# Attention and routed feed-forward on one core: probabilities turned by VectorE in 32x32 blocks, value product in pieces on 32x64 tiles

## The chip, the core and the metric

The kernel runs on 1 core of one Trainium2 chip. The metric is the time of the whole program on the device in microseconds (us), the median of several runs. In the profile PE is TensorE (products; PEld is its weight loads), DVE is VectorE, ACT is ScalarE, POOL is GpSimd and SP is SyncE, which issues the transfers (DMAs).

## What is computed

The input is x of shape (4, 1024, 256) in float32: four batches of 1024 tokens. One attention layer and one routed feed-forward layer (FFN) are applied, each to the layer-normalized x and added to it. The change concerns the attention:

```
q = x @ Wqa @ Wqb                      # 16 heads of 192 = 128 + 64 (rope)
ckv = x @ Wkva                         # 64 latent + 64 rope columns, shared by the heads
kv = compressed @ Wkvb                 # per head 128 key and 128 value columns
q_pe, k_pe = _rope(q_pe), _rope(k_pe)  # o1 = x1*cos - x2*sin, o2 = x1*sin + x2*cos
scores = qf @ kf^T / sqrt(192), causal
attn = softmax(scores)
out = (attn @ v) @ Wout
```

## The kernel before, in words

**Stages.** `attention_prepare` makes keys, latent values and weights of all batches and stores what doesn't fit (0 to 71 us of the span). `attention` runs from 71 to 1231 us. `ffn` runs from there to the end. The change touches the attention and the hand-over to the FFN.

**Folded weights.** The key and value weights are folded into the queries' and the output weights, so a head's queries are 128 numbers (64 latent, 64 rope), and its values are the 64 latent numbers of a token, the same for all heads. Matrices that need more than one pass of precision are split into a high and a low part: a score product is three products (qh with kTh, qh with kTl, ql with kTh).

**Pairs and bodies.** The work goes by pairs of heads: 8 pairs in each of 4 batches, 32 pairs. `run(r)` on each engine is the body of pair r; bodies go from -1 to 32, the last (LAST = 32) being the tail. A pair's queries are split into two halves c (512 tokens each) and two heads a. Half c=0 sees 4 blocks of 128 keys at most, half c=1 sees 8. In a body every engine does a list of jobs in an order written out by hand (TENSOR, VECTOR, SCALAR, POOL, and FIRST and LAST versions for the first body and the tail). The engines meet by semaphores. `age` tells which pair a job in body r belongs to: queries of half 0 are made for pair r+1; turned probabilities, value product and output of half 1 belong to pair r-1.

**Jobs of a pair**, with the lines of the profile:
- Q (4): queries of a half and head, 2 products of 512 columns (L1202). ROT on DVE: one product with cosT (L1369) and two of 32 partitions each with sinT, which swap the rope halves by reading 32 partitions and writing 32 others (L1371). ADD on POOL sums them (L1454); HIGH on ACT makes qh (L1299), LOW on POOL makes ql (L1461).
- S (16): the scores of a tile of 128 queries against w keys, w = 128, 256, 384, 512 in half 0 and 640, 768, 896, 1024 in half 1, so 2560 and 6656 columns, 9216 in all per pair (L1219). MAX on DVE adds the mask and takes the row minimum of the negated scores (L1357), in place in PSUM. EXP on ACT writes `probs` and the row sums (L1307).
- T: TensorE turns `probs` in 128x128 blocks against the identity, 72 blocks per pair (L1233), into 3 PSUM banks, and OUT copies them to `pT` in SBUF (24 copies per pair, 15 by ACT, L1318, and 9 by DVE, L1382).
- PV: the value product in tiles of 128 rows by 64 columns, the two heads side by side (L1253): 24 products per pair of up to 512 columns, each two records in the profile. Half 1 goes in two parts, half 0 in one.
- INV, spread_inverses and O: DVE inverts the row sums and turns them (L1389, L1392). SP writes them to DRAM in 4 small transfers (L1107) and reads them back spread over partitions in 2 (L1111). DVE multiplies the value product by them (L1400); OHIGH (L1325) and OLOW (L1468) split the result.
- Y (4) and ACC (4): the output product, 6 products of 256 columns each (L1266), added to `acc` by DVE (L1409).

**PSUM.** Scores, queries and output products share banks 0 to 3, turned probabilities banks 4 to 6, the value product bank 7.

**Transfers.** SP also loads weights of the next pair, keys and values of batches 2 and 3, and moves `acc` out and in by halves at a batch's end. Toward the end it loads the first expert weights; POOL splits them into high and low (`split_first_quad`, L633, L635).

## Time and profile before

| | us |
|---|---|
| median of 3 runs (1732.09 to 1732.58) | 1732.47 |
| the profiled execution's own time | 1732.48 |
| its span | 1730.7 |
| PE busy | 1662.5 (96%) |
| DVE busy | 1248.5 (72%) |
| ACT busy | 955.1 (55%) |
| POOL busy | 509.9 (29%) |

The profiled execution ran like the timed ones, and 1.8 us of it lie outside the span. Busy times are unions of an engine's records. A TensorE record holds the time from its start to its last result, so consecutive records overlap, and what a product costs is the distance of two starts. An engine that is not the bottleneck may be idle at no cost. Stretches are given in us from the start of the span.

### The profile page before, as it was taken

The page shows a single profiled execution, that of the slowest core. Times are in us where ns is not written, and L with a number is a line of the kernel's source. Part 1 is how long each engine was busy: PE and PEld are TensorE (multiplying, and loading weights), DVE is VectorE, ACT ScalarE, POOL GpSimd, SP SyncE. Part 2 cuts the span into 40 slices and gives each one's busy share as a digit, 9 for nine tenths or more (in the row PEclk, how much of TensorE's full clock was granted, in tenths as well). Part 3 has the DMA queues.
Part 4 walks back from the last instruction along what each step waited for, and adds up shares of the span by engine and source line. Part 5 has one row for each costly group of instructions (what it writes and reads, how often), then busy time and mean ns, then how long its engine had stood idle before and what let it go on. Part 6 is the DMA issues. An engine that isn't in the chain of part 4 may idle for free.

```text
span 1730.7 us, 31809 instructions
## 1 busy us (share of the span) xinstructions
PE 1662.5 (96%) x11024; PEld 1357.5 (78%) x11024; DVE 1248.5 (72%) x2923; ACT 955.1 (55%) x2255; POOL 509.9 (29%) x433
## 2 busy tenths in 40 slices
PE   5799999999999999999999999999999999999998
PEld 4667777777777777777777777777699999999998
DVE  6888888888888788888888888888654554555543
ACT  6566666666666666666666666666433333433332
POOL 4543334323333333423343333335310110110100
PEclk9899999999999999999999999999999999999999
DMA  8300010012000003000002210001300000000000
GB/s 287 117 26 20 20 32 25 20 47 96 20 25 20 20 32 111 26 20 26 25 26 65 65 32 24 22 19 38 110 1 25 26 1 25 26 14 12 13 13 13
DMA packets 50204, 68.49 MB, mean 40 GB/s; under 512 B 8512, under 2 KB 33088, under 8 KB 50048
## 3 DMA queue, kind: packets, MB, share of 16 engines
q1 hardware_dynamic: 50048, 66.45, 11.6%
q8 instruction: 93, 1.52, 0.4%
q14 instruction: 63, 0.52, 0.1%
HBM read 52.00 MB, written 14.42 MB: 38 GB/s over the span
## 4 chain that ended last, share of the span: by engine, by line
PE 81%; issue 8%; DVE 4%; ACT 2%; DMA 1%; POOL 1%; ACTq 0%; DVEq 0%
PE aps L43 46%; PE fps L43 23%; PE aps L1233 9%; PE fps L1618 2%; ACT probs L1307 1%; DVE f_stats L739 1%; DMA raw_down<-in_down 1%; DVE nmax L1357 0%; POOL rot L1454 0%; PE fps L700 0%; PE fps L668 0%; DVE aTl L1759 0%; DVE rot L1371 0%; DVE aps L1357 0%; DVE rot L792 0%
## 5 line engine op out<-in xcount | busy, mean ns | idle before, releaser
L1307 ACT ACTIVATE probs<-aps,nmax 128x384 f32<-128x384 f32 (+7 forms) x512 | 378.6, 743 | 229.7 <-DVE nmax L1357 224.0
L1357 DVE CUSTOM_DVE_ANT_0 aps<-aps,mask_row 128x384 f32<-128x384 f32 (+7 forms) x512 | 387.2, 772 | 105.9 <-PE aps L43 100.3
L1233 PE MATMUL aps<-ident,probs 128*128 128x128 f32 x2304 | 324.0, 272 | 0.9 <-ACT probs L1307 0.6
L43 PE MATMUL aps<-kTh,qh 128*128 128x512 f32 (+3 forms) x768 | 293.3, 382 | 23.3 <-ACT probs L1307 18.4
L1233 PEld LDWEIGHTS aps<-ident,probs 128*128 128x128 f32 x2304 | 271.7, 140 | 27.2 <-issue 1.5
L1318 ACT COPY pT<-aps 128x512 f32<-128x512 f32 (+3 forms) x485 | 229.5, 504 | 92.1 <-PE aps L1233 89.5
L43 PE MATMUL aps<-pT,v 128*64 128x512 f32 (+3 forms) x1536 | 268.9, 492 | 0.6 <-ACT pT L1318 0.6
L43 PE MATMUL aps<-kTl,qh 128*128 128x512 f32 (+3 forms) x768 | 257.9, 343 | 0.0
L1454 POOL TENSOR_TENSOR rot<-rot 64x512 f32<-64x512 f32 x128 | 163.9, 1280 | 211.8 <-DVE rot L1371 211.8
L43 PE MATMUL aps<-kTh,ql 128*128 128x512 f32 (+3 forms) x768 | 221.8, 343 | 0.0
L43 PEld LDWEIGHTS aps<-pT,v 128*64 128x64 f32 x1536 | 101.7, 136 | 152.1 <-issue 142.1
L1461 POOL TENSOR_TENSOR ql<-rot,qh 128x512 fp32r<-128x512 f32 x128 | 164.9, 1288 | 158.5 <-ACT qh L1299 158.5
L43 PEld LDWEIGHTS aps<-kTh,qh 128*128 128x128 f32 x768 | 145.7, 190 | 74.4 <-issue 57.9
L1468 POOL TENSOR_TENSOR ol<-o,oh 128x512 fp32r<-128x512 f32 x64 | 82.3, 1286 | 352.8 <-ACT oh L1325 352.8
L1702 ACT CAST aTh<-fps 128x512 fp32r<-128x512 f32 (+1 forms) x96 | 52.9, 552 | 236.1 <-PE fps L1618 236.0
L1759 DVE TENSOR_TENSOR aTl<-fps,aTh 128x512 fp32r<-128x512 f32 (+1 forms) x96 | 62.0, 647 | 167.3 <-ACT aTh L1702 167.3
L43 PE MATMUL fps<-wth,qh 128*128 128x352 f32 x512 | 176.1, 344 | 2.0 <-PEq L833 2.0
L1371 DVE TENSOR_TENSOR rot<-aps,sinT 32x512 f32<-32x512 f32 x256 | 174.2, 680 | 3.5
L43 PE MATMUL fps<-wtl,qh 128*128 128x352 f32 x512 | 166.3, 325 | 0.0
L43 PE MATMUL fps<-wth,ql 128*128 128x352 f32 x512 | 166.2, 325 | 0.0
L43 PEld LDWEIGHTS aps<-kTl,qh 128*128 128x128 f32 x768 | 146.7, 191 | 9.5
L43 PEld LDWEIGHTS aps<-kTh,ql 128*128 128x128 f32 x768 | 136.7, 190 | 8.2
(190 smaller groups left out, 2878.1 us busy)
## 6 DMA issues: line engine op xcount, KB each, us to landing
linv_b<-inverses_scratch SPq DMA_DIRECT2D x128, 128.0 KB, 2.8
wqs<-wq_scratch SPq DMA_DIRECT2D x30, 256.0 KB, 3.1
raw_numbers<-in_x SPq DMA_DIRECT2D x8, 512.0 KB, 6.2
acc<-in_x SPq DMA_DIRECT2D x8, 512.0 KB, 4.0
inverses_scratch<-linv_t SPq DMA_DIRECT2D x256, 1.0 KB
x_scratch<-acc SPq DMA_DIRECT2D x8, 512.0 KB, 2.9
x<-x_scratch SPq DMA_DIRECT2D x8, 512.0 KB, 3.9
out<-x SPq DMA_DIRECT2D x7, 512.0 KB, 2.9
```

Source lines behind the costliest of these rows:

```text
L43: return nc.tensor.matmul(out, lhsT, rhs, start=start, stop=stop, skip_group_check=True)
L1233: last = nc.tensor.transpose(tps[:, TS.index(x) % 3, j * P:(j + 1) * P], probs[c][:, c * (pair % 2), a, off:off + P], t.ident[:])
L1307: nc.scalar.activation(probs[c][:, c * (r % 2), a, off:off + w], sps[:, at:at + w], ACT.Exp, bias=nmax[:, c, a, j:j + 1], scale=-1.0, accu ...
L1318: nc.scalar.copy(pT[:, k % PT_BUFS, s:QC], tps[:, k % 3, s:QC]).then_inc(t_sb["scalar"], 1)
L1357: nc.vector.tensor_tensor_reduce(out=s, in0=s, in1=mask[:, N - PW[c][j]:N], scale=-1.0, scalar=3.0e38, op0=ALU.add, op1=ALU.min, accum_out ...
L1371: last = nc.vector.tensor_tensor(rot2[to:to + 32, k, :], sps[source:source + 32, at:at + QC], t.sinT[to:to + 32, cols], ALU.mult)
L1454: nc.gpsimd.tensor_tensor(rot1[0:64, k, :], rot1[0:64, k, :], rot2[:, k, :], ALU.add).then_inc(q_add, 1)
L1461: nc.gpsimd.tensor_tensor(ql[:, a, cols], rot1[:, k, :], qh[:, a, cols].bitcast(F32), ALU.subtract).then_inc(q_split, 1)
L1468: nc.gpsimd.tensor_tensor(ol[:, cols], o32[:, c, :], oh[:, cols].bitcast(F32), ALU.subtract).then_inc(o_low, 1)
L1618: last = nc.tensor.transpose(turned_in(i, q)[:, (m - 4 * q) * P:(m - 4 * q + 1) * P], act_sb[:, i % 2, m * P:(m + 1) * P], t.ident[:])
L1702: nc.scalar.copy(aTh[:, i % 2, m.start:m.stop, :].rearrange("p m n -> p (m n)"), turned_in(i, q)[:, 0:len(m) * P]).then_inc(aT_h, 1)
L1759: nc.vector.tensor_tensor(aTl[:, i % 2, m.start:m.stop, :].rearrange("p m n -> p (m n)"), turned_in(i, q)[:, 0:len(m) * P], aTh[:, i % 2, ...
```

## The change

All of `attention` is written anew around these parts; its core is in the diff below.
- **Turning.** T and OUT are gone. After EXP, DVE turns the tile of probabilities in 32x32 blocks (TURN, one instruction per score tile, 16 per pair, 9216 columns). Block b of 32 keys lands in `pT[c][:, a, b, :]` with key k of the block on partition 32g+k, where g tells which 32 of a tile's 128 queries the block holds. `probs` is a ring of 5 tiles, `pT` has one buffer per half for both heads.
- **Value product.** PV runs over blocks of 32 keys. Each block is 8 products: 4 row groups g by 2 heads, with 32 rows, 64 columns of weights and up to 128 columns of moving data. 16 blocks in half 0 and 32 in half 1 give 384 products per pair in place of 24. The result takes 4 banks (4 to 7), one per row group. The values lie four times in SBUF (`vrep`), loaded from DRAM by 4 transfers per batch in runs of 256 bytes. PV(1) is now one stretch, in 4 jobs, and PV(0) in 2.
- **Rope.** ACT copies the queries from PSUM (RAW), SP swaps the two halves of 32 partitions by two transfers (SWAP), and POOL does both multiplications and the sum (ROT). DVE has no part in it.
- **Order.** New lists for all engines, one list for the first body too, SP's jobs in a list of their own (SYNC), and all 8 banks shared by scores, queries and outputs.
- **acc** has two buffers, a whole batch each; it is stored and loaded whole.
- **First expert weights** are split by ACT (high) and DVE (low) in the tail, not by POOL.

```
-KB = [4, 8]
-PT_BUFS = 12
+S32 = 32
+BLOCKS = [16, 32]
+PARTS = [2, 4]
+RING = 5
+OB = 4
...
-                sp.dma_start(t.v_dram[b - 2], t.v32[:, b % 2]).then_inc(kq_stored[b % 2], 16)
+                sp.dma_start(t.v_dram[b].rearrange("(t p) d -> p t d", p=P), t.v32[:, b % 2]).then_inc(kq_stored[b % 2], 16)
...
+        TENSOR = [Q(1, 0), S(0, 1, 0), S(0, 0, 1), Q(1, 1), S(0, 0, 0), S(0, 1, 1), S(0, 1, 2), Q(0, 1), S(0, 1, 3),
+                  Y(0, 1), S(0, 0, 3), S(0, 0, 2), PV(1, 0), PV(1, 1), PV(1, 2), PV(1, 3), S(1, 0, 3), S(1, 0, 1),
+                  S(1, 1, 0), Q(0, 0), Y(0, 0), S(1, 0, 0), S(1, 1, 3), PV(0, 0), PV(0, 1), S(1, 1, 2), S(1, 0, 2),
+                  S(1, 1, 1), Y(1, 0), Y(1, 1)]
+        VECTOR = [MAX(0, 1, 1), MAX(0, 1, 0), MAX(0, 1, 2), MAX(0, 0, 0), MAX(0, 1, 3), ACC(0, 1), INV(1),
+                  TURN(0, 1, 1), TURN(0, 1, 0), MAX(0, 0, 3), MAX(0, 0, 1), TURN(0, 1, 2), MAX(0, 0, 2), INV(0),
+                  TURN(0, 0, 0), TURN(0, 0, 3), TURN(0, 0, 1), O(1), TURN(0, 1, 3), TURN(0, 0, 2), MAX(1, 0, 3),
+                  MAX(1, 0, 1), MAX(1, 1, 0), TURN(1, 0, 3), ACC(0, 0), MAX(1, 0, 0), TURN(1, 1, 0), MAX(1, 1, 3),
+                  TURN(1, 0, 1), TURN(1, 0, 0), TURN(1, 1, 3), O(0), MAX(1, 1, 2), MAX(1, 0, 2), MAX(1, 1, 1),
+                  ACC(1, 0), TURN(1, 0, 2), ACC(1, 1), TURN(1, 1, 2), TURN(1, 1, 1)]
+        POOL = [ROT(1, 0), LOW(1, 0), ROT(1, 1), LOW(1, 1), ROT(0, 1), ROT(0, 0), OLOW(1), LOW(0, 1), LOW(0, 0),
+                OLOW(0)]
+        SYNC = [SWAP(1, 0), SWAP(1, 1), KEEP(1), SPREAD(1), KEEP(0), SPREAD(0), SWAP(0, 1), SWAP(0, 0)]
...
+        TENSOR_FIRST = TENSOR
...
+            def swap(x, r):
+                k = rot_slot(x, r)
+                sp.wait_ge(q_raw, count(of("raw", x), r))
+                sp.dma_start(rot2[0:32, k, :], rot1[32:64, k, :]).then_inc(q_swapped[k], 16)
+                sp.dma_start(rot2[32:64, k, :], rot1[0:32, k, :]).then_inc(q_swapped[k], 16)
...
+            def load_values(b):
+                for a in range(4):
+                    sp.dma_start(vrep[32 * a:32 * a + 32, b % 2], t.v_dram[b].rearrange("(n k) d -> k n d", k=S32))\
+                        .then_inc(values_loaded[b % 2], 16)
...
+                if r == 0:
+                    sp.wait_ge(t.values_stored, 32)
+                    for b in (0, 1):
+                        load_values(b)
+                        load_acc(b)
...
+                if r % PAIRS == 0 and r > 0:
+                    b = r // PAIRS - 1
+                    sp.wait_ge(y_added, last_of("acc", 1, r - 1))
+                    sp.wait_ge(y_added, last_of("acc", 0, r - 1))
+                    sp.dma_start(x2_v[b], acc[:, 1 - b % 2]).then_inc(x2_stored, 16)
+                    if b + 2 < B:
+                        sp.wait_ge(x2_stored, 16 * (b + 1))
+                        load_acc(b + 2)
...
+                def pv_job(x):
+                    _, c, part = x
                     pair = r + age(x)
...
+                        pe.wait_ge(p_turned, last_of("tr", c, pair))
+                        banks_free(x)
+                    n = BLOCKS[c] // PARTS[c]
+                    for b in range(part * n, (part + 1) * n):
+                        s = max(0, b // 4 - 4 * c) * S32
+                        for a in range(4):
+                            for h in range(2):
+                                last = mm(nc, banks[64 * h:64 * h + 64, OB + a, s:4 * S32],
+                                          vrep[32 * a:32 * a + 32, pair // PAIRS % 2, b, :],
+                                          pT[c][32 * a:32 * a + 32, h, b, s:], b == 0, b == BLOCKS[c] - 1)
...
+                def raw_job(x):
+                    _, c, a = x
+                    act.wait_ge(q_ps, count(Q(c, a), r))
...
+                    nc.scalar.copy(rot1[:, rot_slot(x, r), :], banks[:, bank_of(Q(c, a), r), :]).then_inc(q_raw, 1)
...
+                def turn_job(x):
+                    _, c, a, j = x
+                    w = PW[c][j]
+                    dve.wait_ge(e_done, count(EXP(c, a, j), r))
+                    if r > 0:
+                        dve.wait_ge(pv_done, last_of("p", c, r - 1))
+                    nc.vector.transpose(pT[c][:, a, 0:w // S32, j * S32:(j + 1) * S32],
+                                        probs[:, SLOT[EXP(c, a, j), r], 0:w].rearrange("p (b k) -> p b k", k=S32))\
+                        .then_inc(p_turned, 1)
...
-                def add_job(x):
+                def rot_job(x):
                     _, c, a = x
...
+                    pool.wait_ge(q_swapped[k], 32 * ((count(of("raw", x), r) + 1) // 2))
+                    nc.gpsimd.tensor_tensor(rot2[:, k, :], rot2[:, k, :], t.sinT[:, cols], ALU.mult).then_inc(q_turned, 1)
+                    nc.gpsimd.tensor_tensor(rot1[0:64, k, :], rot1[0:64, k, :], t.cosT[0:64, cols], ALU.mult)\
+                        .then_inc(q_turned, 1)
+                    pool.wait_ge(q_turned, 2 * n)
                     nc.gpsimd.tensor_tensor(rot1[0:64, k, :], rot1[0:64, k, :], rot2[:, k, :], ALU.add).then_inc(q_add, 1)
```

## Rows read from the trace of the kernel before

**Rows 1.** The page: busy time of the engines; chain that ended last, by line.

```profile
PE 1662.5 (96%) x11024; PEld 1357.5 (78%) x11024; DVE 1248.5 (72%) x2923; ACT 955.1 (55%) x2255; POOL 509.9 (29%) x433
PE aps L43 46%; PE fps L43 23%; PE aps L1233 9%; PE fps L1618 2%; ACT probs L1307 1%; DVE f_stats L739 1%; DMA raw_down<-in_down 1%; DVE nmax L1357 0%; POOL rot L1454 0%; PE fps L700 0%; PE fps L668 0%; DVE aTl L1759 0%; DVE rot L1371 0%; DVE aps L1357 0%; DVE rot L792 0%
```

**Rows 2.** Stretches: length, busy us (records) of PE, PEld, DVE, ACT, POOL; granted clock, DMA.

```profile
390.85:532.98 142.13, 139.07 (x897) 106.56 (x897) 116.59 (x252) 90.53 (x213) 50.95 (x41) 1.00 0.13 42
...
71.30:106.90 35.60, 27.31 (x136) 20.48 (x137) 28.62 (x65) 18.25 (x45) 16.53 (x15) 0.86 0.18 54
```

**Rows 3.** TensorE in order of time in one period: start us, length us, records.

```profile
501.07 0.60 PE L1233 MATMUL aps<-ident,probs 128*128 128x128 f32 x4
...
506.20 3.65 PE L43 MATMUL aps<-pT,v 128*64 128x512 f32 x16
...
516.59 2.38 PE L43 MATMUL aps<-pT,v 128*64 128x512 f32 x16
...
528.50 2.37 PE L43 MATMUL aps<-pT,v 128*64 128x512 f32 x16
```

**Rows 4.** Groups of DVE, 390.85 to 532.98 us: count, busy us, mean ns, idle before.

```profile
L1357 DVE CUSTOM_DVE_ANT_0 aps<-aps,mask_row 128x896 f32<-128x896 f32 (+6 forms) x64 | 48.4, 772 | 13.3 <-PE aps L43 12.7
L1371 DVE TENSOR_TENSOR rot<-aps,sinT 32x512 f32<-32x512 f32 x32 | 21.8, 680 | 0.4
L1382 DVE COPY pT<-aps 128x384 f32<-128x384 f32 (+3 forms) x36 | 17.6, 507 | 0.1
L1409 DVE TENSOR_TENSOR acc<-aps,acc 128x512 f32<-128x512 f32 x16 | 11.1, 692 | 1.9 <-PE aps L43 1.6
L1369 DVE TENSOR_TENSOR rot<-aps,cosT 128x512 f32<-128x512 f32 x16 | 10.9, 679 | 1.0 <-PE aps L43 1.0
...
L1400 DVE TENSOR_TENSOR o<-aps,linv_b 128x512 f32<-128x512 f32 x8 | 5.5, 692 | 8.3 <-PE aps L43 8.3
L1392 DVE STREAM_TRANSPOSE linv_t<-linv 128x32 f32<-128x32 f32 x8 | 1.7, 212 | 0.3
L1389 DVE RECIPROCAL linv<-lsum 128x8 f32<-128x8 f32 x8 | 1.6, 198 | 0.1
```

**Rows 5.** Groups of DVE by form, whole span: one-source copies and casts.

```profile
L1382 DVE COPY pT<-aps 128x512 f32<-128x512 f32 x64 | 43.7, 683 | 0.0
L1382 DVE COPY pT<-aps 128x128 f32<-128x128 f32 x31 | 8.7, 280 | 0.0
L787 DVE CAST soft_h<-mask_row 128x256 fp32r<-128x256 f32 x8 | 2.4, 294 | 0.3
```

**Rows 6.** Group of PE by form, whole span: products on four row groups (FFN).

```profile
L43 PE MATMUL fps<-mw,xq 32*128 32x352 f32 x256 | 27.7, 423 | 0.0
```

**Rows 7.** TensorE in order of time: products on four column groups, in the tail.

```profile
1225.32 0.80 PE L43 MATMUL aps<-wth,mu 128*32 128x352 f32 x8
```

**Rows 8.** Groups of ACT, 390.85 to 532.98 us.

```profile
L1307 ACT ACTIVATE probs<-aps,nmax 128x896 f32<-128x896 f32 (+6 forms) x64 | 47.3, 743 | 28.9 <-DVE nmax L1357 28.1
L1318 ACT COPY pT<-aps 128x512 f32<-128x512 f32 (+3 forms) x61 | 29.1, 506 | 11.3 <-PE aps L1233 10.9
```

**Rows 9.** Groups of POOL, 390.85 to 532.98 us.

```profile
L1461 POOL TENSOR_TENSOR ql<-rot,qh 128x512 fp32r<-128x512 f32 x16 | 20.6, 1289 | 20.4 <-ACT qh L1299 20.4
L1454 POOL TENSOR_TENSOR rot<-rot 64x512 f32<-64x512 f32 x16 | 20.5, 1280 | 26.3 <-DVE rot L1371 26.3
L1468 POOL TENSOR_TENSOR ol<-o,oh 128x512 fp32r<-128x512 f32 x9 | 11.6, 1287 | 55.0 <-ACT oh L1325 55.0
```

**Rows 10.** SP's transfers of the inverses, 400 to 536 us: issue in ns, landing.

```profile
L1107 SPq DMA_DIRECT2D inverses_scratch<-linv_t x32: 263/295/689, 403.8 to 534.1; - x32
L1111 SPq DMA_DIRECT2D linv_b<-inverses_scratch x18: 450/520/603, 402.6 to 535.8; - x18
...
DMA to landing us min/median/max: 2.7/2.8/3.4
```

**Rows 11.** TensorE in order of time: the first score product of the attention.

```profile
77.55 0.69 PE L43 MATMUL aps<-kTh,qh 128*128 128x384 f32 x1 [4.22 <-POOL ql L1461]
```

More of the change, by code:

```diff
@@ L885, in S, with PV @@
             return ("s", c, a, j)
[L887 to L894 removed]
+        def PV(c, part):
+            return ("p", c, part)
         def Y(c, i):
@@ L903, in EXP, with TURN, RAW, SWAP @@
             return ("exp", c, a, j)
-        def OUT(c, kb, a):
-            return ("out", c, kb, a)
+        def TURN(c, a, j):
+            return ("tr", c, a, j)
+        def RAW(c, a):
+            return ("raw", c, a)
+        def SWAP(c, a):
+            return ("sw", c, a)
         def ROT(c, a):
             return ("rot", c, a)
-        def ADD(c, a):
-            return ("add", c, a)
         def HIGH(c, a):
@@ L921, in INV, with KEEP, SPREAD @@
             return ("inv", c)
+        def KEEP(c):
+            return ("spw", c)
+        def SPREAD(c):
+            return ("spr", c)
         def O(c):
@@ L985, in R @@
+        TENSOR_FIRST = TENSOR
+        VECTOR_FIRST = VECTOR
+        SCALAR_FIRST = SCALAR
+        POOL_FIRST = POOL
+        SYNC_FIRST = SYNC
+        BANK_FIRST = BANK
+        AFTER_EXPERTS = [x for x in VECTOR if x[0] == "max" and x[1] == 1][2]
         def R(part):
@@ L1014, in exists, with body @@
             return 0 <= r + age(x) < B * PAIRS
-        BODIES = range(-1, B * PAIRS + 1)
-        def body(order, first, r):
+        BODIES = range(-1, LAST + 1)
+        def body(order, first, last, r):
+            if r == LAST:
+                return last
             return [x for x in (first if r == 0 else order) if exists(x, r)]
         def tensor_body(r):
-            return body(TENSOR, TENSOR_FIRST, r)
-        TS = [x for x in TENSOR if x[0] == "t"]
-        PVS = [x for x in TENSOR if x[0] == "p"]
@@ new lines, in attention, with of @@
+        SS = [x for x in TENSOR if x[0] == "s"]
+        COUNT, KINDS = {}, {}
+        for bodies in (tensor_body, vector_body, scalar_body, pool_body, sync_body):
+            for r in BODIES:
+                for x in bodies(r):
+                    if x[0] not in ("router", "mask", "stats", "quad"):
+                        KINDS[x[0]] = KINDS.get(x[0], 0) + 1
+                        COUNT[x, r] = KINDS[x[0]]
+        def count(x, r):
+            return COUNT[x, r]
+        def of(kind, x):
+            return (kind,) + x[1:]
@@ new lines, in at_pair, with last_of, slot_before @@
+        def at_pair(x, pair):
+            return count(x, pair - age(x))
+        def last_of(kind, c, pair):
+            return max(at_pair(x, pair) for x in TENSOR + VECTOR + SCALAR if x[0] == kind and x[1] == c)
+        RING_USERS = [(x, r) for r in BODIES for x in scalar_body(r) if x[0] == "exp"]
+        SLOT = {y: n % RING for n, y in enumerate(RING_USERS)}
+        def slot_before(x, r):
+            n = RING_USERS.index((x, r))
+            return RING_USERS[n - RING] if n >= RING else None
@@ L1069, in bank_users, with takes_banks @@
+        def takes_banks(x):
+            return x[0] in ("s", "q", "y", "router", "mask") or x[0] == "p" and x[2] == 0
+        USERS = {bank: [(x, r) for r in BODIES for x in tensor_body(r) if takes_banks(x) and bank in banks_of(x, r)]
+                 for bank in range(8)}
         def bank_users(x, r):
@@ L1295, in high_job @@
                     pair = r + age(x)
-                    act.wait_ge(q_add, count(Q(c, a), r))
+                    act.wait_ge(q_add, count(ROT(c, a), r))
                     if pair > 0:
-                        act.wait_ge(s_ready, count([y for y in SS if y[1:3] == (c, a)][-1], pair - 1))
-                    nc.scalar.copy(qh[:, a, c * QC:(c + 1) * QC], rot1[:, QS.index(Q(c, a)) % 2, :]).then_inc(q_high, 1)
+                        act.wait_ge(s_ready, max(at_pair(y, pair - 1) for y in SS if y[1:3] == (c, a)))
@@ L1350, in max_job @@
                     _, c, a, j = x
-                    at = slot(S(c, a, j), r) + place(c, j)
-                    if r == 0 and x == next(y for y in VECTOR_FIRST if y[0] == "max"):
+                    at = at_of(S(c, a, j), r)
+                    if r == 0 and x == next(y for y in vector_body(0) if y[0] == "max"):
                         dve.wait_ge(mask_loaded, 16)
@@ L1440, in run @@
                         router_vector(nc, t, 0, 0, None)
-                    if r == LAST - 1 and x == MAX(1, 1, 2):
+                    if r == LAST - 1 and x == AFTER_EXPERTS:
                         router_experts(nc, t)
@@ L1477, in run @@
                         router_norm(nc, t, 1, i)
-                for x in body(POOL, POOL_FIRST, r):
+                job = {"rot": rot_job, "low": low_job, "olow": olow_job, "stats": stats_job}
+                for x in pool_body(r):
                     job[x[0]](x)
-                    if r == LAST - 1 and x == LOW(1, 0):
-                        pool.wait_ge(q_ps, max(count(Q(1, a), LAST - PAIRS - 1) for a in range(2)))
+                    if r == LAST - 1 and x == [y for y in pool_body(r) if y[0:2] == ("low", 1)][-1]:
+                        pool.wait_ge(q_ps, max(at_pair(Q(1, a), LAST - PAIRS - 1) for a in range(2)))
                         router_root(nc, t, 0)
```

493 lines of the change are left out of this document (196 added, 297 removed).

## The prediction

> **What bounds the kernel now.** I read the page first: TensorE is busy for 96% of the span, DVE for 72%, and the chain that ended last lies on TensorE's attention products and its turning line L1233 [rows 1]. That points at TensorE, but it is an average over three stages, so I then took a stretch of whole pairs. Four periods lie between 390.85 and 532.98 us, 35.53 us each. In them TensorE is busy 139.07 of 142.13 us, DVE 116.59, ACT 90.53, POOL 50.95, at full granted clock [rows 2]. Per pair that is 34.8 us of TensorE, 29.1 of DVE, 22.6 of ACT, 12.7 of POOL. TensorE idles 0.77 us a pair: it is the bound, and what leaves it shows in the time until the next engine is full. DVE is next, only 6.4 us below the period. About 31 periods repeat this way; the first body and the tail differ.
>
> **TensorE, removed: the turning.** Four blocks span 0.60 us where one lasts 272 ns [rows 3], so a block costs (0.60 - 0.27) / 3 = 0.109 us; 72 a pair are 7.9 us.
>
> **TensorE, changed: the value product.** Its three stretches span 3.65, 2.38 and 2.37 us [rows 3]; less the overlap of each with its successor (about 0.1), 8.2 us. The columns are 9216, two products at a time, so 4608 steps of 1.78 ns. The rest of TensorE's pair is 34.8 - 7.9 - 8.2 = 18.7 us (scores, queries, output) and stays. New, the 384 products have 8 x 1280 + 8 x 3328 = 36864 columns; eight at a time that is again 4608 steps, so 8.2 us. This is the lower end. No row shows eight tiles at once, but four row groups do run together: 256 products in groups of four are busy 27.7 us, 0.433 us a group, where one lasts 0.423 [rows 6]; so the four start within about 10 ns. Four column groups too: 8 records of 352 columns in 0.80 us [rows 7], where eight in a row at 0.8 ns a column would need 2.3. The upper end is that each of the 768 records costs the 0.109 us of a whole turning block: 84 us. I stay near the lower end, since rows 6 and 7 are the nearest, and add 1.3 us for the narrow pieces: the last 16 blocks of each half have 128, 96, 64 and 32 columns, and a 32-column piece (27 ns of streaming a record) can't hide eight starts and weight loads. PV is then 9.5 us, TensorE 28.2 us.
>
> **DVE.** Removed: rope (21.8 + 10.9) and copies 17.6, together 50.3 us in four periods [rows 4], 12.6 a pair. 16.6 us stay, MAX (48.4 / 4 = 12.1) above all. Added: 16 turns of 9216 columns. The trace has this operation only for 32 columns, 212 ns [rows 4]. A one-source copy goes from 280 ns at 128 columns to 683 at 512 [rows 5], 1.05 ns a column. A turn of w columns is so 212 + 1.05 (w - 32): 16 x 178 ns + 9216 x 1.05 ns = 2.8 + 9.7 = 12.5 us. Lower end: SBUF to SBUF at the rate of the cast, 294 ns for 256 columns [rows 5], which leaves about 0.5 ns a column, 7.5 us. Upper end: each 32x32 block costs the full 212 ns, 61 us. I take 12.5, since the copy is the same kind of stream, and no row shows the cast's rate for a turn. DVE is then 29.1 us a pair, as busy as now, but the fullest engine. (The Trainium skill's page "VectorE: DVE Perf Modes", section on the three transpose paths, gives 311 ns for a 128x128 bf16 turn; as an estimate from it and the 212 ns, 1.03 ns a column and 12.4 us. No row here shows a turn of that width.)
>
> **ACT, POOL, SP.** ACT loses 29.1 / 4 = 7.3 us of copies [rows 8] and gains 4 RAW of about 0.6: 17.8 us. POOL gains two multiplications for each ADD, 8 x 1.28 = 10.2 us [rows 9]: 23.0 us. SP issues 8 more transfers a pair at some 0.3 us, landing 2.8 us later [rows 10]; they stand behind the waits of KEEP and SPREAD. All three fit under 31 us, so I cost them nothing in steady state. Their cover is DVE's fullness.
>
> **Period.** DVE needs 29.1 us and TensorE 28.2. TensorE now reaches 98% because the others have slack; two engines this close, in fixed orders, with probabilities in a ring of 5, wait for one another. I take 94% for DVE: 31.0 us. Gain 4.53 x 31 = 140 us.
>
> **Once only.** *Start:* a first score now waits for rope on DVE and one POOL sum, and comes at 77.55 after 4.22 us of TensorE idle [rows 11]. It will wait for RAW 0.6, two issues and landing 3.4, two ROT of 3.84 on POOL (the second queued ahead of LOW) and LOW 1.3, some 7 us more. The granted clock over this body is 0.86 [rows 2], so part of it ran at 1.2 GHz, after TensorE had waited; more waiting keeps it there longer. The first value product also waits for 1024 runs of 256 bytes in each of four transfers, which SP issues only after its jobs of the body. I take +11 us in all (between +3 and +25). *Batch ends:* in bodies 8 and 16 SP waits for the last ACC, stores, waits for the landing (2.8) and loads, and the next SWAP is queued behind; +5 for both (0 to 12). *Tail:* 52 blocks are not turned, -5.6 us; the expert split moves from POOL to ACT and DVE and lies beside the value product, nothing (up to +4). The FFN is unchanged.
>
> **Sum**, against the profiled execution's 1732.48 us (span 1730.7 and 1.8 outside; the median of the runs is the same within 0.01): 1732.5 - 140.4 + 11 + 5 - 5.6 = **1602.5 us**, 7.5% less.
>
> **Rivals.**
> 1. *The query chain holds the body.* Queries of half 1 are made in the body that uses them: Q, RAW, SWAP, three POOL operations, HIGH, LOW come to 0.6 + 3.4 + 3.8 + 0.6 + 1.3 = 9.7 us for the first head, and 5.2 us more on POOL for the second. TensorE's work ahead of S(1,1,0) is about 14 us. There is hardly slack, and SP may be in SPREAD when the swap is due. For it: POOL goes from 36% to 74% of a period. Against: with DVE as bound TensorE is late anyway. Price 2.5 us a pair, 33.5 us: 1732.5 - 63 + 10.4 = 1680.
> 2. *Only four products in flight*, as rows 6 and 7 show and no row exceeds. PV takes 9216 x 1.78 = 16.4 us, TensorE 35.1, the period about 35.9: 1732.5 + 11 + 10.4 = 1754, slower. It decides from PV = 15.7 us on (35.53 - 0.77 - 18.7, less 0.3 for the start).
> 3. *A start costs more than the streaming.* If a record of 32 rows costs a quarter of the 0.109 us of a whole block, 27 ns, PV is 768 x 0.027 = 21 us, the period about 40.5: 1732.5 + 154 + 10 = 1897. The 10 ns for four starts [rows 6] speak against it, but these are bursts of four, not 512 in a row. The turning point is 20 ns a record. Here belongs the rule of the Trainium skill's page "TensorEngine Tiling (Array Packing)", section Performance Considerations, that each matmul has some 60 cycles of overhead: as an estimate 25 ns a record, 19.2 us, and 1842 us in all. By that rule the change loses; rows 6 shows four starts in less than one such overhead.
> 4. *Turning is slower than a copy.* At 2 ns a column TURN is 21 us, DVE 38, the period about 39: 1732.5 + 107 + 10 = 1850. It decides from 18.6 us on, 1.7 ns a column.
> 5. *No net gain*: several delays together use up the 140 us.
>
> **How the numbers follow.** A measurement of this kernel can tell about 0.2% from no change. Forecast 0.60, rival 1 0.22, rival 2 0.05, rival 3 0.05, rival 4 0.04, rival 5 0.04. Faster 0.60 + 0.22 = 0.82, same 0.04, slower 0.14. The forecast's own range is 1565 to 1640. The low end of the whole range is a period of 29.4 us, DVE without a gap: 1732.5 - 190 + 10 = 1552. The high end reaches past rival 1, a period of 34.3: 1732.5 - 38 + 10 = 1705. Rivals 2 to 4 stay outside, 0.14.
>
> **What would show it.** Right: a period near 31 us; DVE over 90% busy in it with 16 turns of 9216 columns in 12 to 13 us; TensorE 75 to 92%; the value product of half 1 spanning 6 to 7.5 us and of half 0 under 3.5. Wrong: a value product over 12 us, with starts of records at an even distance whatever their columns (rival 3) or at twice the streaming time (rival 2); turns of 1024 columns far from 1.25 us (rival 4, or below it a gain); TensorE idle behind POOL's ql (rival 1); granted clock under 1 in the middle of the attention.

## The result and the profile after

The changed kernel takes **1989.04 us** (median of 4 runs, 1983.5 to 1995.41) beside 1732.4 us for the kernel before on the same chip: a ratio of 1.148 (95% interval 1.145 to 1.152). The forecast was 1602.5 us and 7.5% less; it is 14.8% more, above the whole range (1552 to 1705). The profiled execution took 1987.38 us, its span is 1985.6.

From the page of the kernel after (parts 1, 2, 3 and 5, beside [rows 1]); in part 5 the columns are busy us and mean ns, then idle time just before and what ended it:

```profile
span 1985.6 us, 72308 instructions
PE 1614.7 (81%) x31760; PEld 1434.3 (72%) x31760; DVE 1176.2 (59%) x2772; ACT 803.5 (40%) x1902; POOL 812.4 (41%) x681
...
PEclk9889889887998988898889889888889999999999
q8 instruction: 252, 4.13, 0.9%
...
L46 PE MATMUL aps<-pT_second,vrep 32*64 32x128 f32 (+1 forms) x16384 | 255.1, 265 | 182.9 <-issue 174.0
L46 PE MATMUL aps<-pT_first,vrep 32*64 32x128 f32 (+3 forms) x8192 | 120.9, 255 | 87.0 <-issue 78.0
```

No engine is full: TensorE 81%, VectorE 59%. What is new is in the last two rows. In front of the value product TensorE idles 182.9 + 87.0 us, and "issue" ended nearly all of it: neither data nor a semaphore was waited for. The kernel has 72308 instructions (31809 before), and the queue that brings instructions moves 252 packets and 4.13 MB (93 and 1.52 before).

Four periods of the body, against [rows 2]:

```profile
606.30:770.65 164.35, 132.27 (x3489) 115.58 (x3488) 107.44 (x233) 71.45 (x168) 90.21 (x72) 0.91 0.13 35
```

A period is 41.1 us (before 35.5, forecast 31.0). VectorE's 26.9 us, ScalarE's 17.9 and POOL's 22.6 a period are what the change promised, so the parts moved off TensorE arrived where they should. TensorE is the one that is late, and its granted clock is 0.91 where it was 1.00.

TensorE's timeline shows why. One whole value product of half 1 and what follows it (start, length, shape of the first record, count of records; in brackets the idle time before):

```profile
735.13 3.08 PE L46 MATMUL aps<-pT_second,vrep 32*64 32x128 f32 x198 [0.22 <-ACT probs L1331]
739.27 2.06 PE L46 MATMUL aps<-pT_second,vrep 32*64 32x128 f32 x128 [1.06 <-issue]
742.74 1.72 PE L46 MATMUL aps<-pT_second,vrep 32*64 32x96 f32 x128 [1.41 <-issue]
746.21 1.13 PE L46 MATMUL aps<-pT_second,vrep 32*64 32x32 f32 x58 [1.75 <-issue]
747.27 0.80 PE L46 MATMUL aps<-kTh,qh 128*128 128x512 f32 x1
747.86 0.63 PE L46 MATMUL aps<-kTl,qh 128*128 128x512 f32 x1
748.29 0.63 PE L46 MATMUL aps<-kTh,qh 128*128 128x512 f32 x1
```

After the first 198 records the product runs in bursts of exactly 128, and they start 3.47 us apart (739.27, 742.74, 746.21), although the records of the first of them have 128 columns and those of the second 96 and 64. A burst is 128 products and 128 weight loads: 256 instructions. A packet of the instruction queue is 16384 bytes, and 159 more packets for 40499 more instructions are 255 instructions each. In the trace three packets of this queue start at 736.93, 740.39 and 743.81 us, as far apart as the bursts, and each takes about 1 us. The gaps keep their place in the code and not in the work: in five bodies in a row the first one of half 1 stands behind 168, 178, 188, 198 and 208 records. So a burst is a packet, and TensorE eats one in about 2 us and waits for the next. 3.47 us is the shortest of 76 such distances in the run, the median is 4.0. The value product shown takes 12.1 us in half 1 (735.13 to 747.27) and 5.3 in the half 0 before it (716.17 to 721.50); over the four periods it is 18.5 us a pair, of which 7.1 are gaps, where I had put 9.5. (The Trainium skill's page "Vector Engine (DVE) Microarchitecture Reference", section on instruction fetch and dispatch, says that an instruction has 64 bytes; 2.61 MB more for 40499 more instructions are 64.4 bytes, which agrees.)

The last two rows show the second loss. Scores of 512 columns start 0.43 us apart (747.86, 748.29), where they are 0.23 apart after a stretch without gaps (below): 1.2 GHz instead of 2.4, for 3 to 10 us at a time behind or in a value product, in every body. Of the 41.1 us, 18.5 are value product, 18.7 the rest at full clock (the term of the prediction), 0.7 other idle time (32.1 - 29.2 us of issue, over four); so the lower clock takes some 3 us a pair outside the value product. The clock is at 1.2 GHz for 7.7 us a pair in these periods, which can't cost more than 3.8.

```profile
731.41 0.40 PE L46 MATMUL aps<-kTh,qh 128*128 128x512 f32 x1
731.64 0.40 PE L46 MATMUL aps<-kTl,qh 128*128 128x512 f32 x1
```

Over the run: the first maximum comes 8.6 us later than before (the first score product 6.2), the 31 distances from one body's first maximum to the next sum to 1330.2 us (before 1093.1), and what follows is 9.3 us longer; 8.6 + 237.1 + 9.3 = 255.0, the difference of the spans within 0.1. In what follows "the period" is the median of these 31 distances: 41.7 us after, 35.5 before.

VectorE's turns came as worked out:

```profile
L1389 DVE STREAM_TRANSPOSE pT_second<-probs 128x1024 f32<-128x1024 f32 x8 | 9.8, 1222 | 0.0
L1389 DVE STREAM_TRANSPOSE pT_first<-probs 128x128 f32<-128x128 f32 x8 | 2.2, 269 | 0.0
```

### The profile page after: what moved, and what is told of

It reads as the page before. It is cut to its first block, busy times and chain, and to the rows that moved or that the text cites. A ratio compares the mean times of both kernels' runs of the same rounds, so it can differ in the third digit from the quotient of the medians.

```text
span 1985.6 us, 72308 instructions
## 1 busy us (share of the span) xinstructions
PE 1614.7 (81%) x31760; PEld 1434.3 (72%) x31760; DVE 1176.2 (59%) x2772; ACT 803.5 (40%) x1902; POOL 812.4 (41%) x681
## 3 DMA queue, kind: packets, MB, share of 16 engines
q8 instruction: 252, 4.13, 0.9%
## 4 chain that ended last, share of the span: by engine, by line
PE 64%; issue 16%; DVE 11%; DMA 3%; ACT 2%; POOL 1%; SPq 0%; ACTq 0%; DVEq 0%
PE aps L46 41%; PE fps L46 20%; DVE aps L1379 4%; DVE pT_second L1389 3%; PE fps L1632 2%; DVE acc L1423 2%; ACT probs L1331 1%; DMA wqs<-wq_scratch 1%; DMA x_scratch<-acc 1%; DVE nmax L1379 0%; DMA vrep<-values_scratch 0%; DVE f_stats L754 0%; DMA raw_down<-in_down 0%; PE fps L715 0%; PE fps L683 0%
## 5 line engine op out<-in xcount | busy, mean ns | idle before, releaser
L1331 ACT ACTIVATE probs<-aps,nmax 128x256 f32<-128x256 f32 (+7 forms) x512 | 375.0, 740 | 499.3 <-DVE nmax L1379 497.9
L1379 DVE CUSTOM_DVE_ANT_0 aps<-aps,mask_row 128x256 f32<-128x256 f32 (+7 forms) x512 | 376.2, 768 | 157.4 <-PE aps L46 156.4
L46 PE MATMUL aps<-pT_second,vrep 32*64 32x128 f32 (+1 forms) x16384 | 255.1, 265 | 182.9 <-issue 174.0
L1471 POOL TENSOR_TENSOR rot<-rot,sinT 64x512 f32<-64x512 f32 x128 | 162.5, 1270 | 550.5 <-DMA rot<-rot 550.5
L46 PEld LDWEIGHTS aps<-pT_second,vrep 32*64 32x64 f32 x16384 | 232.6, 135 | 211.5 <-issue 208.4
L1389 DVE STREAM_TRANSPOSE pT_second<-probs 128x768 f32<-128x768 f32 (+3 forms) x256 | 254.5, 1023 | 0.3 <-ACT probs L1331 0.3
L1411 DVE TENSOR_TENSOR o<-aps,linv_b 128x512 f32<-128x512 f32 x64 | 44.2, 691 | 319.8 <-PE aps L46 319.8
L46 PE MATMUL aps<-pT_first,vrep 32*64 32x128 f32 (+3 forms) x8192 | 120.9, 255 | 87.0 <-issue 78.0
L46 PEld LDWEIGHTS aps<-pT_first,vrep 32*64 32x64 f32 x8192 | 111.0, 137 | 104.7 <-issue 95.4
L1472 POOL TENSOR_TENSOR rot<-rot,cosT 64x512 f32<-64x512 f32 x128 | 162.8, 1272 | 0.0
```

The costliest lines, as they stand in the source:

```text
L46: return nc.tensor.matmul(out, lhsT, rhs, start=start, stop=stop, skip_group_check=True)
L1331: nc.scalar.activation(probs[:, SLOT[x, r], 0:w], sps[:, at:at + w], ACT.Exp, bias=nmax[:, c, a, j:j + 1], scale=-1.0, accum_out=lsum[:, c ...
L1379: nc.vector.tensor_tensor_reduce(out=s, in0=s, in1=mask[:, N - PW[c][j]:N], scale=-1.0, scalar=3.0e38, op0=ALU.add, op1=ALU.min, accum_out ...
L1389: nc.vector.transpose(pT[c][:, a, 0:w // S32, j * S32:(j + 1) * S32], probs[:, SLOT[EXP(c, a, j), r], 0:w].rearrange("p (b k) -> p b k", k ...
L1411: nc.vector.tensor_tensor(by_token(o32[:, c, :]), banks[:, OB:OB + 4, 0:4 * S32].rearrange("p a (j i) -> p a j i", j=4), by_token(linv_b[: ...
L1471: nc.gpsimd.tensor_tensor(rot2[:, k, :], rot2[:, k, :], t.sinT[:, cols], ALU.mult).then_inc(q_turned, 1)
```

## Experiments

The theories. **A**: TensorE gets its code at 256 instructions per 3.47 us; the value product's 1536 instructions a pair outrun that. **B**: the 27 ns a record are what a record costs to start, wherever it stands (rival 3 of the prediction). **C**: too few products run at once, so streaming bounds (rival 2). **D**: the orders of the other engines set 41 us. Further experiments take up the rope, the ends of the batches, and a version that keeps the gain. A single run of the changed kernel can lie 6 us from its median, so differences under that are not read.

**e_few: 8 of 48 blocks.**

```
 for b in range(part * n, (part + 1) * n):
+    if b > 0 and b % n < n - 1:
+        continue
```

> The value product keeps 8 of its 48 blocks a pair (the first of each half and the last of each part); the other 40 are left out, so it has 256 TensorE instructions instead of 1536. Theory A (code fetch: TensorE gets 256 instructions per 3.47 us in the value product): PV falls from 17.4 to about 3.5 us a pair, the granted clock stays at 1.0, VectorE becomes the bound at 94% and the period is 30 to 32 us, the time 1600 to 1660 us. Rival D (the written order of VectorE, POOL and the transfers sets 41 us, not PV): the period stays 39 to 41 us, the time above 1900 us.

Measured: 1628.31 us, the period 30.3 us. Windows of four periods, and the page's instruction queue (packets, MB, share):

```profile
442.70:564.50 121.80, 95.14 (x930) 77.74 (x929) 106.49 (x235) 71.13 (x168) 90.46 (x72) 0.90 0.16 45
```

```profile
q8 instruction: 92, 1.51, 0.4%
```

D falls: with the value product short, the same orders run at 30 us, within 0.7 us of the forecast of 31.0 for the period. Two expectations were wrong. The clock is 0.90 here too; no loss by it shows, and TensorE is busy only 78%. And VectorE isn't the bound: it is busy 87%, not 94%, and the chain that ended last in these four periods lies mostly on the rope, that is on the swap (14%) and the three operations of ROT on POOL (31%):

```profile
by line: DMA rot<-rot 14.3%; POOL rot L1477 10.5%; POOL rot L1473 10.4%; POOL rot L1474 10.3%; ACT probs L1333 9.7%; issue 9.3%; PE aps L46 7.0%; DVE aps L1381 5.7%; DMA inverses_scratch<-linv_t 3.6%; POOL ql L1483 3.1%; SPq L1129 3.1%; ACT
```

**e_half: 24 of 48 blocks.** The edit skips blocks with `b % 4 in (1, 2)`.

> The value product keeps 24 of its 48 blocks a pair (two of every four are left out), 768 instructions instead of 1536. Theory A (code fetch, 13.6 ns an instruction): PV takes 768 x 13.6 = 10.4 us less what is fetched ahead, TensorE 27 to 29 us, the period 32 to 35 us, the time 1680 to 1790 us. Rival C (only four products in flight, PV bound by streaming 9216 columns at 1.78 ns): PV 8.2 us and 33 to 34 us: not told apart here but by e_narrow. Rival D (orders of the other engines): above 1900 us.

Measured: 1655.8 us, better than the range given; the period is 31.6 us, 156 instruction packets. From 256 to 768 instructions a pair the kernel grows by 27 us, from 768 to 1536 by 333: up to some point the code is there ahead of time or the rope chain covers the wait, from there each instruction is paid for.

**e_narrow: every product, 32 columns each.**

```
+                        e = 4 * S32 if b == 0 else s + S32
...
-                                last = mm(nc, banks[64 * h:64 * h + 64, OB + a, s:4 * S32],
+                                last = mm(nc, banks[64 * h:64 * h + 64, OB + a, s:e],
...
-                                          pT[c][32 * a:32 * a + 32, h, b, s:], b == 0, b == BLOCKS[c] - 1)
+                                          pT[c][32 * a:32 * a + 32, h, b, s:e], b == 0, b == BLOCKS[c] - 1)
```

> All 384 products of a pair stay, but each has 32 columns (the first block of each half keeps 128); the other columns are left out, so streaming falls to 27% of 36864 columns with the same 1536 instructions. Theory A (code fetch): the value product of half 1 still spans 11 to 12.5 us, of half 0 4.5 to 5.5 us, in bursts of 128 records 3.4 to 3.5 us apart, each burst shorter (about 1 us) and the gap longer; the time within 3% of after, 1930 to 2010 us, if anything the clock is lower. Rival C (streaming, four in flight or fewer): PV falls to about a third, the period to 31 us, the time to about 1620 us. Rival B (each record costs 27 ns to start): PV as in A but with starts at an even distance inside a burst.

Measured: 2004.22 us, 0.8% above after, clock 0.841. The same value product in its timeline:

```profile
741.63 2.31 PE L46 MATMUL aps<-pT_second,vrep 32*64 32x128 f32 x198 [0.23 <-ACT probs L1332]
746.04 2.07 PE L46 MATMUL aps<-pT_second,vrep 32*64 32x32 f32 x128 [2.10 <-issue]
749.51 2.06 PE L46 MATMUL aps<-pT_second,vrep 32*64 32x32 f32 x128 [1.40 <-issue]
753.53 1.12 PE L46 MATMUL aps<-pT_second,vrep 32*64 32x32 f32 x58 [1.96 <-issue]
```

And one burst of an earlier value product of the same run:

```profile
221.04 1.50 PE L46 MATMUL aps<-pT_second,vrep 32*64 32x32 f32 x128 [2.35 <-issue]
```

C falls: with a quarter of the columns the bursts have the same 198, 128, 128 and 58 records, 3.5 to 4.4 us apart, and the time is no shorter. How long a burst is has to be read with the granted clock beside it. The two of 2.07 and 2.06 us run at 1.2 GHz (granted clock 0.50). The one of 221.04 runs at 2.4 GHz (1.00): 128 records of 32 columns in 1.50 us, where 128 of 128 columns at the same clock take 2.06 (739.27 above). So the bursts did get shorter, though not to the 1 us that A had said. At full clock a record with its weight load follows the one before by 10 ns with 32 columns and by 14.4 with 128; eight tiles streaming at the prediction's rate (1.78 ns a column for two records) give 14.2. By these numbers starts bound the narrow pieces and streaming the wide ones. B falls: summed over the widths (14.4, 12.6, 11.5 and 10.6 ns in the kernel after at full clock), 768 records are 10.0 us, an estimate that is close to my 9.5. (The Trainium skill's page "TensorEngine Tiling (Array Packing)", section Performance Considerations, has some 60 cycles a matmul, as an estimate 25 ns; the run shows 10 for a record of 32 columns with its load.)

**e_spread: the same work, products of other kinds between the parts.** On top of e_sp (below): PARTS is [4, 8] instead of [2, 4], and all orders are written anew, of which TensorE's begins

```
-TENSOR = [Q(1, 0), S(0, 1, 0), ..., S(0, 0, 2), PV(1, 0), PV(1, 1), PV(1, 2), PV(1, 3), S(1, 0, 3), ...
+TENSOR = [S(0, 1, 3), Q(1, 0), ..., PV(1, 0), PV(1, 1), S(0, 1, 1), Y(0, 1), S(0, 0, 3), PV(1, 2),
+          PV(1, 3), S(0, 0, 2), S(0, 0, 1), PV(1, 4), Q(0, 1), PV(1, 5), Y(0, 0), PV(1, 6), ...
```

> Nothing is left out. The kernel e_sp with another written order: the value product of half 1 in 8 jobs of 4 blocks, of half 0 in 4 jobs, with scores, queries and output products between them in banks 0 to 3, so that code is fetched while TensorE streams wide products; the other engines' orders follow. Theory A (code fetch of 256 instructions per 3.47 us is a rate; 1888 instructions a pair need 25.6 us of it, so spread over the pair it is hidden; a record of the value product then costs its 16 ns, 12.4 us a pair): no gap over 1 us inside the value product, the period 33.5 to 36 us instead of 41.2, the granted clock at 1.0 in most of a period, the time 1710 to 1790 us. Rival B (27 ns a record is the start cost whether spread or not): 18.7 + 20.9 = 39.6 us of TensorE a pair, the period 40 us or more, no gain over 1956 us. Rival D (the orders of the other engines set 41 us): tells nothing by itself, since they change too, but e_few excluded it.

Measured: 1813.65 us, 143 us below e_sp, though above the range given; the period is 36.3 us, the clock 0.965. Some of the parts now:

```profile
625.00 1.21 PE L46 MATMUL aps<-pT_second,vrep 32*64 32x128 f32 x64
...
628.90 1.08 PE L46 MATMUL aps<-pT_second,vrep 32*64 32x64 f32 x64
...
631.00 0.86 PE L46 MATMUL aps<-pT_second,vrep 32*64 32x32 f32 x64
```

These parts have no gap in front, and a record costs 13 to 19 ns with the last one's whole length counted in (0.86 / 64, 1.21 / 64), so the long time of a record was the code's rate, not the record's. Most bodies take seven packets, at 3.47 us each 24 us of code a pair, and this is nearly hidden when it is spread: over the bodies gaps put down to issue still take 1.5 us a pair, the longest 3.4. In four quiet periods (545.3 to 688.7 us, clock 0.99) TensorE spends 12.4 us a pair on the value product: 10.3 from record to record, and 2.2 where a part ends and the next product starts, eleven times a pair at some 0.2 us. The rest of its work takes 20.2 and idle time 3.2, half of it behind EXP. So the cut into many parts costs back some 2 us of the 6.6 that the change frees on TensorE. What a better order could win back isn't shown.

**e_joint: half the instructions, all the columns.**

```
+                        half = slice(64 * (b % 2), 64 * (b % 2) + 64)
...
-                            for h in range(2):
-                                last = mm(nc, banks[64 * h:64 * h + 64, OB + a, s:4 * S32],
...
+                            out = banks[half, OB + a, 0:8 * S32].rearrange("p (h n) -> p h n", h=2)
+                            last = mm(nc, out[:, :, s:], vrep[32 * a:32 * a + 32, pair // PAIRS % 2, b, :],
+                                      pT[c][32 * a:32 * a + 32, :, b, s:], b < 2, b >= BLOCKS[c] - 2)
```

> The kernel after, but one product takes the columns of both heads (256 where it had 128), and the two halves of TensorE's columns take turns by block: 192 products of 73728 / 2 columns instead of 384, so the same 36864 columns with 768 instead of 1536 instructions. Left out: the sums of the even and of the odd blocks are not joined, and the step behind it reads only a part. Theory A (the number of instructions counts, not the columns): PV takes about 768 x 13.6 = 10.4 us a pair, the period 31 to 33.5 us and the time 1655 to 1730 us, within 4% of e_half (1656), which streams half of these columns. Rival C (streaming counts: only four products in flight): PV 16.4 us as in after, the time above 1900 us.

Measured: 1640.53 us, better than the range given. Windows of five periods, and both value products of one body:

```profile
422.90:575.80 152.90, 140.93 (x2441) 120.58 (x2440) 132.60 (x291) 88.94 (x210) 113.24 (x90) 1.00 0.16 45
```

```profile
609.44 6.07 PE L46 MATMUL aps<-pT_second,vrep 32*64 32x256 f32 x256 [0.22 <-ACT probs L1331]
...
624.63 2.62 PE L46 MATMUL aps<-pT_first,vrep 32*64 32x256 f32 x128
```

All 36864 columns stream in 6.07 + 2.62 = 8.7 us, beside the 8.2 that I worked out as the lower end from [rows 3]. So eight tiles do run at once, and the streaming term was right. The clock in these periods is 1.00 and the period is 31.0 us. This is nearly the time that I had forecast, with all the columns and 768 instead of 1536 instructions. Halving them also halves the starts, but by the distances above that is worth only some 1.3 us a pair (10.0 against 8.7) of the 9.8 by which the value product got shorter. Two things keep it from being the forecast kernel: the sums aren't joined, and VectorE is busy 87%. Of the chain that ended last in these periods 29% are the swap and the three operations of ROT, and 17% VectorE's maxima and turns. VectorE shares the bound with the rope.

**e_sp: one transfer ahead of the waits.** At the end of a batch SP loads the query weights of the body after next before it waits, as the kernel before did.

```
 if r % PAIRS == 0 and r > 0:
+    if 0 < r < LAST:
+        queries_of_second_half(r)
+        load_wq(r + 2)
```

> Only the transfer of the query weights of bodies 9 and 17 is issued before SP's waits at the end of a batch instead of behind them; nothing is left out. Theory: the 11 us that TensorE waits for these weights in bodies 9 and 17 go, 10 to 20 us less than after (1969 to 1979 us). Rival (another wait of the batch end takes their place): within 4 us of after.

Measured: 1956.4 us, 33 us less, more than expected. In the kernel after the wait and SP's queue around it are

```profile
PE aps L46 <- DMA wqs<-wq_scratch: 11.0, 1, 11.0
```

```profile
444.39 8.23 SPq L1143 DMA_DIRECT2D vrep<-values_scratch  x4
464.21 0.38 SPq L1198 DMA_DIRECT2D x_scratch<-acc  x1
468.65 0.39 SPq L1147 DMA_DIRECT2D acc<-in_x  x1
469.09 0.58 SPq L1133 DMA_DIRECT2D wqs<-wq_scratch  x1
```

The edit moves the weights of body 25 too. Bodies 9, 17 and 25 go from 54.8, 50.6 and 47.1 us to 45.5, 43.8 and 40.8, which is 22 of the 33; the rest lies in small amounts over the other bodies and I can't say from what.

**e_late: the transfers of a batch's end two bodies later**, and the values of the first batch in the middle of body 0; on e_spread.

```
-if r % PAIRS == 0 and 0 < r < LAST:
+if r % PAIRS == LATE and LATE < r < LAST:
```

> Nothing is left out. e_spread with SP's transfers moved: keys, queries and values of the next batch and the exchange of x are issued two bodies after a batch's end instead of in the body that ends it, and the values of the first batch in the middle of body 0. Theory: in e_spread the bodies 8, 9, 16, 17, 24 and 25 take some 35 us more than six ordinary ones, and the first value product waits 8.7 us for its values; most of the first (the swaps queued behind SP's waits and issues) and of the second goes: 20 to 40 us less than e_spread, 1775 to 1795 us. Rival (what makes these bodies long is the code fetch beside the load of 2 MB, or the same waits in a later body): under 12 us less.

Measured: 1805.86 us, 8 us less: the rival was right. Bodies 8 and 9 fall from 41.6 and 45.1 to 36.2 and 35.6 us, but body 10 rises to 42.9, and body 19 to 43.3. SP's queue in body 10:

```profile
478.11 6.47 SPq L1146 DMA_DIRECT2D vrep<-values_scratch  x4
484.67 2.61 SPq L1204 DMA_DIRECT2D x_scratch<-acc  x1
493.11 0.39 SPq L1150 DMA_DIRECT2D acc<-in_x  x1
```

The four loads of the values, in runs of 256 bytes, occupy the queue for 6.5 us, and the load of acc waits for the store to land; swaps stand behind both. Where the block stands matters little as long as it is one block.

**e_rope: the rope part alone, on the kernel before.** VectorE's three products of ROT become one copy, SP swaps the halves, POOL does `rot2 * sinT`, `rot1 * cosT` and the sum.

> The kernel before with the rope part of the change alone: VectorE only copies the queries out of PSUM (in after this copy is ScalarE's), two transfers swap the halves, POOL multiplies twice and adds. Turning, copies and value product are those of before. Theory A (rope costs nothing while another engine is the bound; TensorE is busy 98% of a period): the period stays 35.5 to 36 us, the time 1725 to 1755 us (a later first score adds some us). Rival Q (the longer query chain, 3.4 us of transfer and 2.6 us more on POOL for each of four, holds the body): the period 37 us or more, the time above 1780 us.

Measured: 2149.02 us, the period 47.3. My expectation was far off. From the waits of three periods:

```profile
ACT qh L1321 <- POOL rot L1477: 55.9, 12, 7.5
...
POOL rot L1473 <- DMA rot<-rot: 33.8, 6, 8.8
```

ScalarE, in order, stands 55.9 us before HIGH, and behind HIGH stand copies of turned blocks that TensorE needs. In that order a Q has its scores close behind it; the chain of 2.0 us of landing and 2.5 us more of POOL for each of four queries doesn't fit. The change's own order suits it better: there, with the value product short (e_few), the same chain fits in 30 us, though it is then what holds the body. I had costed it at nothing because all engines had room; room is not what a chain needs.

**e_join: e_joint made complete.** ScalarE copies the odd sums out of PSUM, VectorE adds the even ones and multiplies.

```
+                    nc.scalar.copy(odd[64:128], banks[64:128, OB:OB + 4, 0:8 * S32].rearrange("p a (h n) -> p a h n", h=2))\
...
+                    for h in range(2):
...
+                        nc.vector.tensor_tensor(by_token(o32[64 * h:64 * h + 64, c, :]), even,
+                                                odd[64:128, :, h].rearrange("p a (j i) -> p a j i", j=4), ALU.add)\
...
+                    nc.vector.tensor_tensor(o32[:, c, :], o32[:, c, :], linv_b[:, c, :], ALU.mult).then_inc(o_sb, 1)
```

> Nothing is left out: the complete form of e_joint. ScalarE copies the odd sums (64 partitions, 1024 columns, about 1.1 us a half) out of PSUM, VectorE adds the even ones to them (two additions) and then multiplies by the inverses: 2.4 us a pair more on VectorE, 2.2 us on ScalarE, and 1.1 + 0.6 us of chain ahead of each OHIGH. Theory: e_joint's period of about 31 us plus what VectorE gets, 31.5 to 34 us; the time 1660 to 1740 us (1640.5 and 32 times 0.6 to 3.1), so with 4 chances in 5 faster than before (1732). Rival: the longer chain behind the value product (banks 4 to 7 are held 1.7 us longer, the output product comes later) sets the body: 35 us or more, 1770 us or more.

Measured: 1862.1 us, ratio to before 1.076 (1.072 to 1.080): the rival. Its waits over 160 us name the place:

```profile
PE aps L46 <- DVE o L1430: 30.1, 8, 5.9
...
DVE o L1426 <- ACT odd L1344: 23.2, 8, 4.2
```

Twice a body TensorE waits for banks 4 to 7, up to 5.9 us, because the next score in the order needs them.

**e_order and e_order2: e_join with other orders.** Scores behind a value product go to banks 0 to 3, the banks come free after the additions, SP's block is spread over five bodies (one transfer group in each). e_order2 has a further order of the same jobs, and the first values in the middle of body 0.

```
                         elif y[0] == "p":
-                            pe.wait_ge(o_sb, count(O(y[1]), rr))
+                            pe.wait_ge(o_joined, 2 * count(O(y[1]), rr))
```

> Nothing is left out. e_join with three things changed. Its written order: the value products in parts with other products between them, scores behind them in banks 0 to 3, so that TensorE does not stand behind O for banks 4 to 7 (3 to 5 us twice a body in e_join). The banks are given back after the two additions, not after the multiplication. SP's transfers at the end of a batch are spread over five bodies, each behind the swaps. Theory: the waits on O go, and the period is that of the fullest engines (VectorE 29.6 us of work, TensorE 27.5) with gaps: 32 to 35 us; the time 1640 to 1730 us. Rival (the longer chains of joining and rope leave no order in which the engines keep busy): 36 us or more, over 1760 us.

> Nothing is left out. e_order with another written order of the same jobs and with the values of the first batch loaded in the middle of body 0 (before, they came after SP's jobs of that body; the first value product waited 9.0 us for them in e_order). Theory: 0.3 to 0.8 us a period less than e_order's 34.8 and 3 to 8 us less in body 0: 1711 to 1731 us, faster than before (1732) by 0.1 to 1.2%. Rival (with four engines at 60 to 88% of a period the order is no longer worth anything on the chip): within 6 us of e_order, 1738 to 1750 us, no faster than before.

Measured: e_order 1743.89 us, above its range, ratio 1.0062 (1.0045 to 1.0079); e_order2 **1712.83 us**, ratio 0.9884 (0.9867 to 0.9900). The second beats the kernel before by 1.2% and the changed one by 14%. The bodies at the ends of batches are ordinary in e_order (34.3 us each for 8 and 9). Four of e_order2's periods:

```profile
607.30:742.00 134.70, 115.40 (x1943) 93.40 (x1942) 119.92 (x247) 81.02 (x175) 92.22 (x72) 0.98 0.21 57
```

VectorE is busy 30.0 us of 33.7, 89%. Against e_joint's 31.0 us the joining costs 3 us a pair; the start is still dear, body 0 takes 44.5 us (before 26.8).

## Why the prediction was wrong, point by point

- **The step that failed: "I stay near the lower end ... PV is then 9.5 us".** It measured 18.5 us. The sum had no term for bringing the instructions: 1536 of them in two blocks outrun the supply of code, 256 per 3.47 us at best. By its own terms the sum was nearly right: at full clock and with the code at hand the records are 10.0 us by estimate (10.3 in e_spread), so the add of 1.3 us for narrow pieces was some 0.5 short. Of the 9.0 us too little, 7.1 are gaps, and the rest is this half microsecond, the lower clock and what each gap cuts off. The row that could have warned was on the page of before: 31809 instructions came in 93 packets over 1731 us, and the change adds 40000 into the value products of 32 pairs. I counted columns and records, never instructions.
- **Rival 3** comes nearest by number: 27 ns a record, 40.5 us a period, 1897 us. That is luck, since its mechanism, the cost of a start, isn't what happened: at full clock a record takes 10 to 15 ns. The doubt in it, "bursts of four, not 512 in a row", was the right doubt, for another reason than the one written.
- **Granted clock**: the prediction took 1.00 in steady state. It is 0.91, and by the working above some 3 us a pair. That it follows the gaps is what the rows show; no run took the gaps' clock away alone, so the 3 us stay a reading.
- **TensorE, the rest**: 18.7 us and 7.9 us removed hold: 18.7 + 18.5 + 3.2 + 0.7 gives the 41.1 by construction, but e_joint, with 18.7 + 8.7 = 27.4 us, has TensorE busy 28.2 a period at full clock.
- **Streaming of eight tiles, 8.2 us**: right, 8.7 in e_joint. Rival 2 falls.
- **VectorE**: a turn of 1024 columns 1.22 us (1.25 worked out), of 128 columns 269 ns (313), so 12.0 us a pair (12.5). Rival 4 falls. In all 26.9 us a period busy, not 29.1, since operations in a row overlap by some 0.1 us.
- **Period 31.0 because VectorE bounds at 94%**: the number came out where the value product is short, 30.3 in e_few and 31.0 in e_joint, the reason didn't. VectorE is at 87% of a lower sum, and the chain that ended last lies on the rope as much as on it, so that both agree within 0.7 us is in part luck.
- **ACT, POOL, SP costed nothing**: without effect in the kernel after, where the chain that ended last is TensorE and issue for 86% of the four periods. But it isn't true: rival 1's chain is real. It holds the body in e_few at 30 us, below rival 1's 33.5, and in e_rope's order at 47 us (2149 us in all).
- **Start +11**: the first maximum is 8.6 us later and body 0 takes 42.6 us, not 26.8; less the 6.2 us by which every body is longer, that is 18.2 us in all. **Batch ends +5**: bodies 8, 9, 16, 17, 24 and 25 hold 39 us above six ordinary ones. I had priced the landing, not 8 us of issue for runs of 256 bytes nor the weights queued behind. **Tail -5.6**: it came out +9.3; its value product of half 1 meets the same code rate, and the lower clock.

By size, of the 387 us between forecast and result: 31 periods of 41.7 instead of 31.0 are 332, batch ends 34, the tail 15, the start some 7: 388, the same within rounding and the spread of the bodies.

## What to carry to other kernels

Before cutting a product into small tiles, count instructions, not only columns: each piece is a weight load and a product for each pass, and here 256 of them came every 3.47 us at best, while at full clock such a pair took 10 to 15 ns once its code was there. And read a burst's length only beside the granted clock of that very stretch: 2.06 us meant 128 columns at 2.4 GHz and 32 columns at 1.2. Prefer few wide pieces (here both heads in one product, blocks in turns on the two halves of the columns), and put wide products between what small ones are left. And a step that moves to an idle engine is free only if the distance in the written order between its source and its user covers the longer chain.

## What the runs showed of the hardware

- TensorE's code comes in packets of 16384 bytes. In a long run of small products bursts of one packet each start 3.47 us apart at best and 4.0 in the median (76 distances in after), while a packet's own transfer takes about 1 us; what sets the 3.47 us isn't shown. While keys and values are being loaded, packets were 4.7 to 5.7 us apart in e_sp and in after. Between 86 and 249 records with their loads ran before the first gap.
- A record on a 32x64 tile with its weight load follows the one before by 10 ns with 32 columns (128 in 1.50 us, e_narrow) and by 14.4 ns with 128 (128 in 2.06 us, after) at full clock; at 1.2 GHz 128 records of 32 columns take 2.07 us. In e_joint 256 records of 256 columns and fewer, 208 in the mean, take 6.07 us, 24 ns each, which is streaming on eight tiles.
- Around the gaps TensorE runs at 1.2 GHz for 3 to 10 us at a time, and e_few has the clock at 0.90 with 78% busy, at a period of 30.3 us.
- VectorE turns 32x32 blocks of f32 at 1.06 ns a column ((1222 - 269) / 896), the rate of a one-source copy [rows 5].
